# Three-pass fp32r scores in two of five attentions, a four-strip narrow attention, and a new order at the start and in the first attention's last batch

## The reference

```python
# L0: keys are [context, x], 16 heads of 16, masked; then rmsnorm + MLP
# L1, L3: twice  x = x + cross_attention(layer_norm(x), context), 16 heads of 128
#         with one extra bias key and value, then x = x + mlp(layer_norm(x))
logits = einsum('bqhk,bthk->bhqt', qh, kh) / scale
weights = softmax(logits)
ctx = einsum('bhqt,bthk->bqhk', weights, vh).reshape(b, q_len, H * K)
return ctx @ wo + bo
# L2: narrow attention, 16 heads of 16, on the context, then MLP (256 -> 1024 -> 256)
```

## Time and profile before

| | us |
|---|---|
| median of 3 runs | 928.24 (927.35 to 928.96) |
| the profiled execution | 924.61, its span 922.8 |
| TensorE busy | 859.1 (93%) |
| VectorE busy | 630.1 (68%) |
| GpSimd busy | 550.4 (60%) |
| ScalarE busy | 496.9 (54%) |

### The profile page before, as it was taken

How to read it: one execution, slowest core, us unless ns; L and a number is a source line. 1 busy time by engine, 2 the same in 40 slices (tenths; PEclk the granted TensorE clock), 3 DMA queues, 4 the chain that set the end, 5 groups by cost and what they waited for, 6 DMA issues and landing times.

```text
span 922.8 us, 16592 instructions
## 1 busy us (share of the span) xinstructions
PE 859.1 (93%) x5936; PEld 711.8 (77%) x5936; DVE 630.1 (68%) x1329; ACT 496.9 (54%) x1204; POOL 550.4 (60%) x638
## 2 busy tenths in 40 slices
PE   4899977899999999999899898999999999999898
PEld 3677756899966799666798686899966699766798
DVE  3678886518889768897432499418889768898330
ACT  2677767555753357533563344755753357533562
POOL 2678884577943469564295053577853369564393
PEclk8899999999999999999999999999999999999999
DMA  6843212002550025200001100202550024100001
GB/s 192 278 125 104 92 40 104 1 1 92 163 215 1 1 69 171 104 1 1 6 19 36 57 1 1 104 1 87 165 217 1 1 69 161 46 1 1 1 13 35
DMA packets 26677, 64.09 MB, mean 69 GB/s; under 512 B 2995, under 2 KB 15843, under 8 KB 25444
## 3 DMA queue, kind: packets, MB, share of 16 engines
q1 hardware_dynamic: 26596, 63.03, 20.7%
HBM read 57.22 MB, written 5.77 MB: 68 GB/s over the span
## 4 chain that ended last, share of the span: by engine, by line
PE 67%; DVE 19%; POOL 4%; issue 4%; DMA 2%; ACT 2%; SPq 1%; DVEq 0%; POOLq 0%
PE ps L1008 7%; PE ps L948 6%; PE ps L909 6%; PE ps L937 5%; PE ps L984 5%; PE ps L734 3%; PE ps L735 3%; PE ps L736 3%; PE ps L715 3%; DVE prob L1699 3%; PE ps L791 3%; PE ps L716 3%; PE ps L717 3%; DVE mx L1698 3%; DVE z L1534 3%
## 5 line engine op out<-in xcount | busy, mean ns | idle before, releaser
L1008 PE MATMUL ps<-arena,pT_all 128*128 128x256 f32 x512 | 116.6, 381 | 5.9 <-DVE x L1719 3.8
L1008 PEld LDWEIGHTS ps<-arena,pT_all 128*128 128x128 f32 x512 | 96.2, 190 | 32.5 <-issue 15.3
L558 POOL TENSOR_TENSOR rstd<-var,neg_half 128x1 f32<-128x1 f32 (+1 forms) x56 | 33.9, 606 | 137.8 <-DVE var L1528 137.8
L984 PE MATMUL ps<-arena,hT 128*128 128x512 f32 x256 | 115.5, 594 | 0.0
L598 POOL TENSOR_TENSOR prob<-prob,rinv 128x512 f32<-128x512 f32 x32 | 49.5, 1548 | 108.7 <-DVE rinv L1712 108.7
L565 POOL TENSOR_TENSOR arena<-arena,rinv 128x640 f32<-128x640 f32 x64 | 80.4, 1258 | 42.1 <-DVE rinv L1513 41.7
L1280 ACT ACTIVATE arena_r<-ps,cols 128x256 fp32r<-128x256 f32 x128 | 66.5, 520 | 55.5 <-PE ps L717 55.3
L619 POOL TENSOR_TENSOR arena_r<-arena,arena_r 128x512 fp32r<-128x512 f32 x64 | 84.0, 1331 | 9.9 <-ACT arena L1281 9.9
L715 PE MATMUL ps<-hH,w1H 128*128 128x256 f32 x256 | 74.9, 293 | 11.9 <-DVE prob L1699 5.2
L1237 ACT ACTIVATE arena<-ps,nb 128x320 f32<-128x320 f32 x128 | 66.3, 524 | 33.5 <-DVE nb L1499 32.8
L1388 ACT ACTIVATE prob<-prob 128x512 f32<-128x512 f32 x32 | 20.2, 631 | 116.2 <-DVE prob L1699 116.2
(11 more groups left out here) (176 smaller groups left out, 2459.1 us busy)
## 6 DMA issues: line engine op xcount, KB each, us to landing
ring<-in_heads_dram SPq DMA_DIRECT2D x64, 512.5 KB, 3.4
w<-in_w_dram SPq DMA_DIRECT2D x8, 1024.0 KB, 8.0
first_r<-spare_k SPq DMA_DIRECT2D x24, 160.0 KB
first_q<-spare_q SPq DMA_DIRECT2D x48, 64.0 KB, 2.5
spare_k<-HL SPq DMA_DIRECT2D x8, 320.0 KB, 2.5
spare_q<-HL SPq DMA_DIRECT2D x8, 256.0 KB, 2.5
x<-in_x_dram SPq DMA_DIRECT2D x1, 1024.0 KB, 6.1
lnb<-in_lnb_dram SPq DMA_DIRECT2D x4, 256.0 KB, 6.8
```

The lines of the kernel that those rows point to most:

```text
L984: last = mm(ps[:, SCORES[k][half], :], hT[:, k, d, 0:P], A[:, d, b // 2, cols_of, sl, :].rearrange("p r s k -> p r (s k)"), start=(d == 0) ...
L1008: last = mm(ps[:, 6, 0:D], pT[:, k, c, :], VW[:, b, c, :], start=(c == 0), stop=(c == PAIRS - 1))
```

## The change

**Start.** SP loads kinT of sequence 0 and the k half of w0 first, then the q half, cols, and soon kinT of sequence 1. TensorE multiplies ones by ones seven times before the first product and four times before the rounds; base(4) and base(5) move ahead of the rounds. VectorE splits the first two results before it makes the masks.

**Last batch of attend0.** ScalarE copies every odd round from round 48 on; the norms of mlp0's first rows are taken one row at a time in rounds 49, 51, 53, 55.

**keys0 and keys2, tokens0 and tokens2.** A is kept as two fp32r parts: ScalarE writes the high part, VectorE subtracts (A_low) and no longer copies VW, whose lower half ScalarE copies. h gets a second copy in fp32r and its rest (`tile_low`). Scores are three passes of fp32r products. A_low lies over w1, w2, w1H and w2H, so the weights of layers 1 and 3 are loaded behind head 4 of keys1 and keys3, after a wait for all scores of the tokens before. In these two stages ScalarE copies the turned softmax between the two exponentials, and VectorE adds an earlier tile's output before it sums.

**attend2.** Heads are 16 rows in strips of 32 with two heads each; K is written twice, zeroed for one head of the two in turn. Scores are 8 products in four strips of 32 rows, on four banks, ahead of them 4 products of a row of ones with the mask. The sums take 128 columns; VectorE inverts them, and 8 products of 32x32 corners spread the inverses (`inverses`), which ScalarE copies. The query bias moves to ScalarE, the statistics of all tiles ahead of the loop, and the maximum and difference run in two halves. `project` has 6 jobs, and only the last waits for mlp1's last add. The loop has one stage more.

```diff
-        BY_ACT = (1, 3, 9, 11)
+        def by_act(i):
+            return i % 16 in (1, 3, 9, 11) or (i >= 48 and i % 2 == 1)
...
-            sp.dma_start(w0, t["w0"]).then_inc(in_base, 16)
             sp.dma_start(kinT[:, :, 0, :], t["kinT"][:, :, 0, :]).then_inc(in_base, 16)
+            sp.dma_start(w0[:, 0, :, :], t["w0"][:, 0, :, :]).then_inc(in_base, 16)
+            sp.dma_start(w0[:, 1, :, :], t["w0"][:, 1, :, :]).then_inc(in_w0q, 16)
...
+            sp.dma_start(kinT[:, :, 1, :], t["kinT"][:, :, 1, :]).then_inc(in_kin1, 16)
...
+                elif l > 0:
+                    sp.wait_ge(s_ps, TILES * (SEQ[l - 1] + 1))
...
                     sp.dma_start(ring[:, n % RING, :], t["heads"][a, h]).then_inc(in_ring[n % RING], 16)
+                    if a % 2 == 1 and h == RING:
+                        load_mlp(a)
...
-            sp.dma_start(kinT[:, :, 1:B, :], t["kinT"][:, :, 1:B, :]).then_inc(in_kin, 16)
+            sp.dma_start(kinT[:, :, 2:B, :], t["kinT"][:, :, 2:B, :]).then_inc(in_kin, 16)
...
+                pe.wait_ge(pool_set, 1)
+                keep_busy(7)
+                pe.wait_ge(in_base, 32)
...
+                pe.wait_ge(in_kin1, 16)
+                pe.wait_ge(hl_ready, 1)
+                base(4)
                 pe.wait_ge(consts_ready, 1)
+                pe.wait_ge(hl_ready, 5)
+                base(5)
+                keep_busy(4)
...
+                    if a % 2 == 0:
+                        pe.wait_ge(h_low, TILES * (a // 2) + g + 1)
+                        passes = ((hH, A_high), (hH, A_low), (hL, A_high))
+                    else:
+                        passes = ((hT, A),)
...
+                    for j in range(4):
+                        at = slice(32 * j, 32 * j + 1)
+                        mm(ps[:, j, 0:D], ones_r[at, :], mask2[at, b * C:(b + 1) * C].unsqueeze(1).broadcast_to([1, 4, C]),
+                           start=True, stop=False)
+                    for m in range(DH):
+                        for j in range(4):
+                            at = slice(32 * j, 32 * j + 32)
+                            last = mm(ps[:, j, m * P:(m + 1) * P], qT2[at, k, m, :], KC[at, m, b, :],
+                                      start=False, stop=(m == 1))
...
+                def inverses(g):
+                    pe.wait_ge(inv2_ready, g + 1)
+                    for m in range(DH):
+                        for j in range(4):
+                            at = slice(32 * j, 32 * j + 32)
+                            last = mm(ps[at, 4, D + m * P:D + (m + 1) * P],
+                                      spread_of[at, m, :, :].rearrange("p e t -> p (e t)"), inv2[at, :], start=True, stop=True)
+                    last.then_inc(inv2_ps, 1)
...
+                for i in range(TILES + 3):
+                    if 3 <= i <= TILES:
+                        inverses(i - 3)
...
+                    if a % 2 == 0:
+                        slots = slice(0, 4, 3) if par == 0 else slice(1, 3)
+                        dve.wait_ge(a_act, n + 1)
+                        v.tensor_tensor(A_low[:, :, :, h // 2, slots, :].rearrange("p d g s k -> p (d g) s k"),
+                                        ps[:, 2 + k, :].rearrange("p (dg s k) -> p dg s k", dg=4, s=2),
+                                        A_high[:, :, :, h // 2, slots, :].rearrange("p d g s k -> p (d g) s k").bitcast(F32),
+                                        ALU.subtract).then_inc(a_low, 1)
...
+            def tile_low(a, g):
+                k = g % 2
+                dve.wait_ge(h_ready, TILES * SEQ[a] + g + 1)
+                v.tensor_tensor(hL[:, k, :, 0:P], hT[:, k, :, 0:P], hH[:, k, :, 0:P].bitcast(F32), ALU.subtract)\
+                    .then_inc(h_low, 1)
...
-                if i == 50:
-                    dve.wait_ge(rows_done, 2)
-                    mlp_spread(0, 0)
-                elif i == 52:
-                    dve.wait_ge(rows_done, 4)
-                    mlp_spread(0, 1)
-                elif i in (56, 58):
-                    mlp_z(0, (i - 56) // 2)
+                if i in (49, 51, 53, 55):
+                    row = (i - 49) // 2
+                    dve.wait_ge(rows_done, row + 1)
+                    last = spread(x0[:, row, :], row // 2, row % 2, True)
```

More of the change, by code:

```diff
@@ L233, in build @@
         in_base = sem("in_base")
+        in_w0q = sem("in_w0q")
+        in_cols = sem("in_cols")
+        in_kin1 = sem("in_kin1")
         in_w1 = sem("in_w1")
@@ L340, in up_slot @@
             if b == 0 and l > 0:
-                bank, half = (((0, 4, 5, 6) if l == 2 else (0, 1, 2, 5))[f // 2], f % 2)
+                bank, half = ((0, 1, 2, 5)[f // 2], f % 2)
             else:
@@ L372, in v0_out, with out2, heads_of @@
             return ps[:, 7 if b else 2, 0:P]
+        def out2(g):
+            return ps[:, 7 if g < 4 else 3, D:2 * D]
+        def heads_of(n, parity):
+            return sum(1 for i in range(n) if i // H % 2 == parity)
         block = ctx.enter_context(nc.Block())
@@ L820, in output, with keep_busy @@
                     last.then_inc(o_ps, 1)
+                def keep_busy(n):
+                    for i in range(n):
+                        mm(ps[:, 6, 0:P], ones[:, :], ones[:, :], start=True, stop=True)
                 def aside(step, b):
@@ L1101, in output @@
                         pe.wait_ge(rows_done, rows_before("L2") + g)
+                    if g < 4:
+                        pe.wait_ge(h_ready, base + g + 6 if g < 3 else base + TILES)
+                    else:
+                        pe.wait_ge(s_used, base + TILES)
                     for d in range(DH):
-                        last = mm(ps[:, 3, 0:D], oT[:, g % 2, d, :], vw2[:, 1, d, :], start=(d == 0), stop=(d == 1))
+                        last = mm(out2(g), oT[:, g % 2, d, :], vw2[:, 1, d, :], start=(d == 0), stop=(d == 1))
                     last.then_inc(o_ps, 1)
@@ L1421, in attend2 @@
                         last.then_inc(pT_act, 1)
+                    if i + 2 < TILES:
+                        scaled(base + i + 2, "L2_ln1_w", "L2_ln1_b")
+                    if i + 1 < TILES:
+                        queries(i + 1)
                     if i < TILES:
@@ L1706, in softmax @@
                         v.tensor_copy(crow[:, :], ps[:, 6, 0:D]).then_inc(crow_ready, 1)
+                    if g >= 2 and a % 2 == 0:
+                        add(g - 2)
                     dve.wait_ge(e_half, 8 * a + g + 1)
```

425 lines of the change are left out of this document (249 added, 176 removed).

## The result

The changed kernel takes 916.84 us, median of 4 runs (915.56 to 920.81), against 928.18 before: ratio 0.9896, 95% interval 0.9869 to 0.9923. Measured again beside other runs of before, it takes 918.79 (6 runs) against 927.57, ratio 0.9913 (0.9897 to 0.993). So the change brings 9 to 11 us, where I had forecast 27. The sign is right and 901 is 16 us too low; 916.84 lies at the slow end of the stated range of 884 to 917, and 918.79 outside it.

What follows compares the result with a forecast made beforehand. It took TensorE to bound tokens and keys, VectorE attend0's end, and transfers the start. 3 + 4 + 14 - 1 - 4.2 + 11.2 = 27 us off 924.61 gives 897.6, as a median 901 us; range 884 to 917.

Steps and rivals of the forecast that it cites:

- 1. Start: Start of attend0: smaller first loads bring brow's landing and what follows forward, 3 us gained, bounds 1 and 4.5.
- 2. Last batch: Last batch of attend0: copies moved from VectorE to ScalarE and single-row sums give 4 us, bounds 0 and 6.
- 3. tokens0, tokens2: Three-pass fp32r scores: VectorE becomes the bound at 7.5 us a tile, 7 us gained each, bounds 4.5 and 8.
- Rival (b): tokens0, tokens2: tile_low at 0.78 and pT copies keep 7.9 us a tile, half the gain remains, 908 us; chance 0.16.
- 14 - 1 - 4.2: Forecast for the three-pass scores: 14 us gained in tokens0 and tokens2, 1 lost in keys0 and keys2, 4.2 in keys1 and keys3.
- 4. keys0, keys2: A_low replaces VectorE's copy of VW, ScalarE takes that copy: 0.5 us lost a stage, bounds 0 and 2.
- rival (d): keys0, keys2: A_low blocks GpSimd, 32 us more, 933 us, slower than before; chance 0.04.
- 5. keys1, keys3: Heads queue behind 2 MB of MLP weights, head 5 lands at 345.2: 2.1 us lost each, bounds 0 and 4.
- 6. attend2: Shorter prologue, about equal tile loop, longer tail: 11.2 us gained in the sum, bounds 1 and 19.
- The loop: attend2's tiles: dependencies sum to 5.9 us a tile, as before; 0.5 us gained in all, bounds -8 and +7.
- The tail: End of attend2: one more stage of the pipeline against an earlier up(0), 0.8 us.
- Rival (a): attend2: the inverses run one by one, 1.3 us more in six tiles, 909 us; chance 0.17.

Runs made afterwards that it cites:

- Run 6: The changed kernel with 13 more dummy products on TensorE at the start of attend0: 919.04 us.
- run 14: The best version with the last batch of attend0 as before the change (four rounds of sixteen on ScalarE, norms two rows at a time): 907.41 us.
- Run 5: The changed kernel with tile_low, norm and statistics behind the first half's maximum and subtraction in tokens0 and tokens2: 920.2 us.
- run 7: The changed kernel with single-pass fp32 scores in tokens0 and tokens2, and the copies and weight loads of before: 918.32 us.
- run 1: The changed kernel measured and profiled again, nothing edited: 918.79 us.
- Run 3: The changed kernel with 15 dummy products on TensorE in tiles 0 and 1 of attend2: 917.21 us.
- Run 8: The changed kernel with output(5) and output(6) directly behind values(6) and values(7) in attend2's end: 914.2 us.
- the best version: The changed kernel with MLP weights behind the last head, attend2 scores ahead of inverses, early tail outputs, dummies in attend2, one brow row first: 904.66 us.
- run 13: The best version with tile_low, norm and statistics behind the first maximum and subtraction in tokens0 and tokens2: 904.03 us.

## Why the prediction was wrong, point by point

**1. Start: mechanism right, size off.** Brow landed at 33.5 us in the profiled execution, as forecast, but of the 3 us that gave only 1.9 arrived at 50 us. Behind the landing TensorE worked at half clock until 42 us (0.53 from 20 to 40 us, 0.71 before). Run 6 could not remove that, but the other traces tell what it costs. From brow's landing to the maximum of round 48 it is 82.1 us before the change, without half clock behind the landing, and 82.1 to 82.2 in the seven traces with 3.4 to 6.0 us of it; then the distance grows with it, 82.4 at 6.4 us, 82.65 at 7.1, 83.0 at 7.8, up to 83.2 at the 8.2 us of the changed kernel's first trace. The 1.1 us between 83.2 and 82.1 are the missing ones. The landing itself scatters by 4 us, which the forecast didn't allow for.

**2. Last batch: right.** up(0, 0) starts at 149.6 instead of 154.5 us, 1.9 of it from the start: 3.0 against a forecast of 4; run 14 gives 3.0 in this stage and 2.7 in the median.

**3. tokens0, tokens2: the term that was mis-sized, 3.5 instead of 7 each.** I asked first what TensorE alone would give and took 0.8 us a tile; 12 products take 2.77 us (2.64 to 2.9 forecast) against 3.44, so 0.67, 5.4 in all. VectorE takes the other 1.9: its tile is 7.77 us, not 7.5, since tile_low takes 1.26 us and not 0.4, while the norm behind it falls from 0.73 to 0.47 in the mean (it had stood behind GpSimd's product before; that place moved, and its price with it). The forecast's upper bound of 0.78 was the mean of another instruction, and the trace of before had a price in this very place:

```profile
278.00 1.55 POOL L598 TENSOR_TENSOR prob<-prob,rinv 128x512 f32<-128x512 f32 x1 [3.39 <-DVE rinv L1712]
278.56 1.13 DVE L1534 TENSOR_SCALAR z<-x,mv,rstd 128x256 f32<-128x256 f32 x1
```

Run 5 shows what this is worth: with tile_low moved, and no clock drop, tokens2 is 1.1 us shorter. And VectorE's three short tiles at the end (6.7, 5.6, 5.2) didn't set the pace: from tile 4 on the chain runs over TensorE at 7.1 us a tile. Rival (b) named tile_low beside GpSimd and half the gain: it is what happened. The 14 - 1 - 4.2 of the sum were 7.0 - 1.6 - 5.9 in the first trace; run 7 shows that nothing is left of them in the changed kernel.

**4. keys0, keys2: right**, 0.8 against 0.5, near the place named: one head takes 4.19 us instead of 3.15, from the VW of head 2 to that of head 3. There ScalarE's copies come on top, GpSimd waits for vpart, and VectorE, without gaps from 216.8 to 221.3 us, also has tile_low of the first two tiles (1.09 us), which the forecast didn't place here. A_low takes 0.69 us; rival (d) is out.

**5. keys1, keys3: right for the gap** (2.1 us, GpSimd waits 2.08 for the DMA), though the terms written there, 335.2 + 6.6 + 2, give a landing at 343.8 and a gap of 0.7, not the 345.2 that was used: from the issue of head 4 to the landing of head 5 it was 10.0 us, and of these the terms hold 8.6. That the gap came true is luck in part. It was wrong for its sequel in keys3: 1.7 us more at half clock. These two stages were forecast without a clock.

**6. attend2: the step that failed, 2.3 instead of 11.2.** From the last sum of mlp(1) to the first maximum of tile 0 it is 11.5 us instead of 22.2 (counted from the start of that sum): -10.7, forecast -9.9. (The terms written there, with the 0.7 us for the last add, give a start of the scores at 513.7 and not 514.3, so -10.5.) From there to the maximum of tile 7: 46.2 instead of 44.2 (45.3 in run 1), forecast -0.5. From there to the norm of mlp(2): 25.6 instead of 19.2 (24.7 in run 1), forecast -0.8. Two terms failed.
The loop (-0.5 forecast, +2.0 measured) was worked out as a sum of dependencies, 5.9 us, and came to 6.27, so that was nearly right; but the maxima of tiles 2 and 3 came 7.2 us behind the ones before, at half clock. TensorE has 2.06 us of work in the 4 us from 509 to 513, since queries, scores and maxima of the first tiles follow one another with nothing beside them; at 512.7 the clock falls to 1.2 GHz and stays there for 13.7 us (10.2 in run 1). Run 3 shows 2.4 to 3.3 us for that: with the dummies the stretch is 42.8 us, 1.4 less than before the change.
The tail is the larger of the two (-0.8 forecast, +6.4 measured). It was "one more stage of the pipeline against an earlier up(0)". It was never laid out queue by queue: up(2, 0), values, inverses and output share TensorE's order, and the longer pipeline lets output(5) wait behind up. Run 8 shows 2.1 us of it. Another 0.9 (25.6 against 24.7 in run 1) stands beside half clock from 560.5 to 563.9 us, which run 1 doesn't have there. The last 3.4 (22.6 against 19.2) are left even in the best version; their cause is open.
Rival (a) is out: the inverses follow each other in 0.57 us, where eight one after the other would be 1.8. The Trainium skill (TensorEngine Tiling (Array Packing), Gotcha 1: PSUM Pressure) says that different row tiles can't access the same bank at once. This trace doesn't agree: the eight products write one bank from four row groups, each on its own partitions, in under a third of the 1.8 us.

**7. tokens1, tokens3: no step named them.** They became 1.4 us longer each in the first trace. At 441 to 444 us TensorE's products of mlp(1) are 0.21 us apart instead of 0.12: half clock again, behind 2 us with 0.3 us of work. In other traces of the same kernel family it was absent (121.8, as in run 3), so it comes and goes.

The sum against medians: 27 forecast; 9 to 11 measured by medians, 3.8 between the two profiled executions. Of the missing 23.2 us between these, the tail of attend2 holds 7.2, its loop 2.5, and tokens0 and tokens2 3.5 each. Before's profiled execution was its best and after's its worst of four, so the ledger makes the change look smaller than it is. Which stages the 5 to 7 us lie in can't be read from one trace each.

## What to carry to other kernels

Work out a new loop's fill and drain as carefully as its period: here the prologue and period were right, and 6 of the 11 us went in the drain, 2 of them shown to lie in the order of one engine's queue. When loads move next to a stream of loads, put them behind the last of the stream. Before splitting a product into cheaper passes, see what the next engine has to prepare for them, and in whose shadow on SBUF it will stand.

## What I had not expected of the hardware

A stretch in which TensorE is half idle costs more than the idle time. Behind 509 to 513 us with 2.06 us of work in 4, the clock was at 1.2 GHz for 14 us; behind a wait of 1.8 us in keys3 for 3 us. Dummy products in such a stretch held 2.4 GHz (0.54 and 0.60 became 1.00), but with other gaps left the clock fell at one of them: alone they gave 1.6 us in the median, within the scatter. In run 13 an edit that freed VectorE came with half clock in both stages, and gave nothing.

Half clock is not always dear: up to 6.0 us of it behind brow's landing cost nothing by round 48, and 8.2 us cost 1.1.
